# Second normalised tile transposed by a SyncE DMA instead of by TensorE, in a gated two-layer kernel on one core

## What is computed

```python
x = x + tanh(g_xattn[0]) * xattn(layernorm(x), token_ids, ctx, ctx, ctx)
x = x + tanh(g_ffn[0]) * ffn(layernorm(x), Wr, br, Wd, bd, Wu, bu)
# xattn: each token goes to one of 4 experts e, by its token id:
#   y = (silu(h @ W[e].T) * (h @ W[e].T)) @ W[e].T,   W = ctx, 4 x 512 x 512
# ffn: 8 experts of rank 16, the best 2 of softmax(h @ Wr + br) mixed:
#   out = sum_e w[e] * (relu(h @ Wd[e] + bd[e]) @ Wu[e] + bu[e])
```

## Time and profile before

| | us |
|---|---|
| median of 3 runs | 203.06 (202.65 to 203.64) |
| span of the profiled execution | 201.4 |
| busy: TensorE, VectorE, ScalarE, GpSimd | 175.0, 155.7, 111.9, 99.7 |
| share of the span: TensorE, VectorE, ScalarE, GpSimd | 87%, 77%, 56%, 50% |

### The profile page before, as it was taken

The page is one execution under the profiler, slowest core; times in us unless marked ns, Lnnn a source line. Parts: engine busy times, 40 slices in busy tenths (PEclk is TensorE's granted clock), DMA queues, the critical chain, the costliest instruction groups (busy, mean ns, idle before and its releaser), DMA issues.

```text
span 201.4 us, 4382 instructions
## 1 busy us (share of the span) xinstructions
PE 175.0 (87%) x1074; PEld 104.0 (52%) x1075; DVE 155.7 (77%) x523; ACT 111.9 (56%) x224; POOL 99.7 (50%) x246
## 2 busy tenths in 40 slices
PE   1576896999997989999999999999999999976560
PEld 1564463655553656656656556655665655534310
DVE  4859696697768799889888998797877878678640
ACT  2596599884287166473665726547265561545200
POOL 4478846427246366375553735516244162445641
PEclk9999999999999999999999999999999999999955
DMA  5947572101210201203101011011010100101121
GB/s 135 370 163 231 205 216 69 52 5 20 86 55 0 52 0 52 59 0 104 55 0 54 0 52 52 2 52 52 0 54 0 52 20 33 52 0 55 52 104 52
DMA packets 6784, 13.43 MB, mean 67 GB/s; under 512 B 2392, under 2 KB 2520, under 8 KB 6768
## 3 DMA queue, kind: packets, MB, share of 16 engines
q0 software_dynamic: 2560, 8.39, 12.6%
q1 hardware_dynamic: 4208, 4.86, 7.3%
HBM read 9.06 MB, written 4.19 MB: 66 GB/s over the span
## 4 chain that ended last, share of the span: by engine, by line
PE 44%; issue 18%; POOL 10%; DVE 9%; DMA 7%; ACT 4%; DVEq 3%; SPq 2%; POOLq 1%; ACTq 0%
PE ps_y L603 6%; PE ps_y L605 6%; PE ps_y L604 6%; PE ps_a L603 4%; PE ps_a L605 4%; PE ps_a L604 4%; DMA xs<-in_x_dram,rows_of 4%; ACT h L796 3%; POOL rs L457 3%; PE ps_h2T L685 2%; PE ps_pT L624 2%; DMA bu_nat<-in_L_ffn_bu_dram 2%; POOL hot_slot L432 2%; PE ps_hT L677 2%; POOL xs L439 2%
## 5 line engine op out<-in xcount | busy, mean ns | idle before, releaser
L456 POOL TENSOR_SCALAR ve<-mv 128x1 f32<-128x1 f32 x32 | 7.7, 239 | 62.6 <-DVE mv L1099 51.8
L796 ACT ACTIVATE h<-xs,mrs,rs 128x512 f32<-128x512 f32 (+1 forms) x16 | 21.1, 1317 | 22.4 <-POOL mrs L458 22.4
L783 ACT ACTIVATE pT_hi<-ps_pT 128x512 f16<-128x512 f32 x19 | 11.3, 595 | 36.0 <-PE ps_pT L624 36.0
L603 PE MATMUL ps_y<-w_hi,pT_hi 128*128 x76 | 28.8, 379 | 2.3 <-DVE w_lo L952 1.5
L603 PE MATMUL ps_a<-w_hi,hT_hi 128*128 x76 | 29.1, 382 | 0.7 <-DVE hT_lo L1074 0.6
L604 PE MATMUL ps_a<-w_lo,hT_hi 128*128 x76 | 29.1, 382 | 0.0
L605 PE MATMUL ps_a<-w_hi,hT_lo 128*128 x76 | 29.0, 381 | 0.0
L604 PE MATMUL ps_y<-w_lo,pT_hi 128*128 x76 | 28.8, 379 | 0.0
L605 PE MATMUL ps_y<-w_hi,pT_lo 128*128 x76 | 28.8, 379 | 0.0
L1086 DVE SCALAR_TENSOR_TENSOR xs<-ps_y,y_t,xs 128x512 f32 x19 | 14.3, 750 | 10.2 <-PE ps_y L605 7.7
L529 POOL DMA_INDIRECT out_dram<-xs,rows_of x16 | 17.3, 1083 | 5.9 <-DVE xs L1117 3.5
(11 more groups left out here) (209 smaller groups left out, 424.0 us busy)
## 6 DMA issues: line engine op xcount, KB each, us to landing
w_nat<-in_ctx_dram SPq DMA_DIRECT2D x4, 1024.0 KB, 7.9
xs<-in_x_dram,rows_of POOLq DMA_INDIRECT x16, 3.6
wd_nat<-in_L_ffn_Wd_dram SPq DMA_DIRECT2D x1, 256.0 KB
wu_nat<-in_L_ffn_Wu_dram SPq DMA_DIRECT2D x1, 256.0 KB
out_dram<-xs,rows_of POOLq DMA_INDIRECT x16, 2.9
b_in<-in_L_ffn_bd_dram SPq DMA_DIRECT2D x1, 64.0 KB
bu_nat<-in_L_ffn_bu_dram SPq DMA_DIRECT2D x3, 16.0 KB
tok_i<-in_itok_BxS_dram SPq DMA_DIRECT2D x1, 8.0 KB, 1.8
```

The costliest lines, as they stand in the source:

```text
L603: mm(ps[:, :], lhs_hi[:, kc, :], hi, start=(kc == 0), stop=False)
L796: a(h2[:, :, :], x1[:, col(k), :].rearrange("p o (q c) -> p c (o q)", c=KC), ACT.Identity, bias=mrs[:, 1, col(k)], scale=rs[:, 1, col(k)]) ...
```

## The change

`h2` is written in token order, as one 512-wide row a token. ScalarE copies it to fp16 into the first half of a new tile `h2_parts`, VectorE writes the rest into the second half; both read SBUF now. A single DMA transpose, issued by SyncE, brings all eight 128 x 128 blocks of `h2_parts` into `h2T`, whose halves are `h2T_hi` and `h2T_lo`. It waits for the lo part, for the hidden product of the tile before (which reads the same `h2T`) and for the landing of the transpose before. The hidden product waits for its landing. TensorE's transposes of h2 go. To match the order, `wr_nat` and `wd_nat` are loaded with rows c*128 + p, `wd_nat` by eight DMAs. In SyncE's loop transpose t - 10 comes behind the `x_in` signal of tile t, from t = 10 on; ten transposes follow the loop.

```diff
-        h2 = sb("h2", [P, KC, P])
-        h2T_hi = sb("h2T_hi", [P, KC, P], fp16)
-        h2T_lo = sb("h2T_lo", [P, KC, P], fp16)
+        h2 = sb("h2", [P, D])
+        h2_parts = sb("h2_parts", [P, 2, D], fp16)
+        h2T = sb("h2T", [P, 2 * KC, P], fp16)
+        h2T_hi, h2T_lo = h2T[:, 0:KC, :], h2T[:, KC:2 * KC, :]
...
+            def transpose_h2(k):
+                sp.wait_ge(h2_lo_done, k + 1)
+                if k:
+                    sp.wait_ge(hid_mm, k)
+                    sp.wait_ge(h2T_landed, 16 * k)
+                sp.dma_start_transpose(h2T[:, :, :], h2_parts[:, :, :].rearrange("p a d -> p (a d)"))\
+                  .then_inc(h2T_landed, 16)
...
-                    sp.dma_start(wr_nat[:, :, :], Wr.rearrange("(p c) e -> p c e", c=KC)).then_inc(s_small, 16)
-                    sp.dma_start(wd_nat[:, :, :, :], Wd.rearrange("e (p c) r -> p e (c r)", c=KC)).then_inc(s_small, 16)
+                    sp.dma_start(wr_nat[:, :, :], Wr.rearrange("(c p) e -> p c e", c=KC)).then_inc(s_small, 16)
+                    for e in range(EF):
+                        sp.dma_start(wd_nat[:, e, :, :], Wd[e, :, :].rearrange("(c p) r -> p c r", c=KC)).then_inc(s_small, 16)
...
+                if t >= 10:
+                    transpose_h2(t - 10)
+            for k in range(T - 10, T):
+                transpose_h2(k)
             sp.wait_ge(s_scatter, 16 * T)
...
-                pe.wait_ge(h2T_lo_done, k + 1)
+                pe.wait_ge(h2T_landed, (k + 1) * 16)
...
-                if some(T, -2 - LATE, i0):
-                    k = i - 2 - LATE
-                    pe.wait_ge(normed2, k + 1)
-                    for c in range(KC):
-                        last = tr(ps_h2T[:, c, :], h2[:, c, :], ident[:, :])
-                    last.then_inc(h2T_done, 1)
...
-                    wait_last(act, h2T_done, k)
-                    a(h2[:, :, :], x1[:, col(k), :].rearrange("p o (q c) -> p c (o q)", c=KC),
+                    wait_last(act, h2_lo_done, k)
+                    a(h2[:, :], flat(x1[:, col(k), :]),
                       ACT.Identity, bias=mrs[:, 1, col(k)], scale=rs[:, 1, col(k)]).then_inc(normed2, 1)
...
-                    act.wait_ge(h2T_done, k + 1)
-                    wait_last(act, hid_mm, k)
-                    a(h2T_hi[:, :, :], ps_h2T[:, :, :], ACT.Copy).then_inc(h2T_hi_done, 1)
+                    act.wait_ge(normed2, k + 1)
+                    if not (isinstance(k, int) and k == 0):
+                        act.wait_ge(h2T_landed, k * 16)
+                    a(h2_parts[:, 0, :], h2[:, :], ACT.Copy).then_inc(h2_hi_done, 1)
...
-                dve.wait_ge(h2T_hi_done, k + 1)
-                v.tensor_tensor(h2T_lo[:, :, :], ps_h2T[:, :, :], h2T_hi[:, :, :],
-                                ALU.subtract).then_inc(h2T_lo_done, 1)
+                dve.wait_ge(h2_hi_done, k + 1)
+                v.tensor_tensor(h2_parts[:, 1, :], h2[:, :], h2_parts[:, 0, :],
+                                ALU.subtract).then_inc(h2_lo_done, 1)
```

More of the change, by code:

```diff
@@ L285, in bass_flamingo_gated_kernel @@
         normed2 = sem("normed2")
-        h2T_done = sem("h2T_done")
-        h2T_hi_done = sem("h2T_hi_done")
-        h2T_lo_done = sem("h2T_lo_done")
+        h2_hi_done = sem("h2_hi_done")
+        h2_lo_done = sem("h2_lo_done")
+        h2T_landed = sem("h2T_landed")
         hid_mm = sem("hid_mm")
@@ L754, in ffn_squares @@
             def ffn_squares():
-                act.wait_ge(s_small, 16 * 8)
+                act.wait_ge(s_small, 16 * (7 + EF))
                 act.wait_ge(s_sq, 1 + E * KC)
@@ L999, in router_bias @@
             def router_bias():
-                dve.wait_ge(s_small, 16 * 8)
+                dve.wait_ge(s_small, 16 * (7 + EF))
                 v.tensor_scalar(b_in[:, ER:HC], b_in[:, ER:HC], BONUS, None, ALU.add)\
```

## The result

The changed kernel takes 255.71 us (median of 4 runs, 253.45 to 257.48) against 203.22 us for the kernel before beside it: a ratio of 1.255 [1.248, 1.262]. The forecast was 256 us. In the rows `h_parts` is the tile `h2_parts`.

What follows compares the result with a forecast made beforehand. TensorE's own work was taken as the main stage's bound, 8.47 us a step. Terms 3.4 + 3.2 + 38.1 + 4.1 + 3.8 = 52.6, plus span 201.4 and 1.6, gave 255.6, say 256 us; range 220 to 335.

Steps and rivals of the forecast that it cites:

- the steps of 11.4 us: Sign in the main stage: hidden products 11.4 us apart, from 7.2 + 0.1 + 4.1, against TensorE's own 8.03.
- loads and first hidden product: Two terms at the front: smaller load pieces shift everything by +3.4 us; the first hidden product waits for its transpose, +3.2.
- thirteen steps: Main stage, first to fourteenth hidden product: 148.2 us instead of 110.1, +38.1 us.
- What bounds: Main stage: TensorE's work is the bound before; the change puts the transfer on its path, with 1.05 us to hide in.
- The step's fixed chain: Main stage, start of one hidden product to end of the next lo part: 7.2 us, plus 0.1 for semaphore hand-overs.
- L, the landing: Time of the transpose DMA from issue to landing, once a tile: 4.1 us, between 1.8 and 7.9.
- The clock: Rival: TensorE's clock falls in the new waits, half or all its path work at 1.2 GHz: 298 or 339 us; chance 0.12.
- Loads: Early stretch: seven more issues on SyncE's queue delay VectorE's router_bias and all behind it, +3.4 us, bounds +1.5 and +6.8.
- Drain: Last two hidden products, 15 and 16, each waiting for its transpose: +4.1 and +3.8 us.
- Eight blocks one after another: Rival: the transfer is served block by block, 1.8 us each, landing in 14.4 us: 420 us; chance 0.12.
- As fast as ordinary transfers: A skill page's claim on transposing DMAs: landing would be the gather's 3.6 us and the time 248 us.
- Hidden transfer, faster: Rival: with a landing under 0.7 us, lo part plus transfer fit in front of TensorE's 8.03 us: 197 us; chance 0.02.

Runs made afterwards that it cites:

- the double transfer: The changed kernel with each transpose sent a second time into a spare tile, the hidden product waiting for both: 287.24 us, run once.
- its control: The kernel before, TensorE's transposes kept, with the hidden product and what follows it one step later and two buffers: 210.37 us, ratio 1.036.
- the split kernel: The changed kernel with two transposes a tile, one of the hi part and one of the lo part, each sent when written: 250.49 us, ratio 1.222.

## Why the prediction was right

The total was right within 0.3 us, and the mechanism held, but that the number fits so well is luck: the landing, which the sum holds sixteen times, was taken 16 us too large in all, and effects that the forecast left out made up for 13.6 of them. Of the signs that it named, TensorE's waits of some 3 us a step and VectorE's wait of 5 came; the steps of 11.4 us came as a mean of 11.2 and at no quiet step, and the full clock did not come. Point by point, in the difference of the two profiled spans (53.9 us):

| term | predicted | measured |
|---|---|---|
| loads and first hidden product | 3.4 + 3.2 | 77.8 - 66.3 = 11.5 |
| thirteen steps | 38.1 | 145.7 - 110.1 = 35.6 |
| drain, two products | 4.1 + 3.8 | (240.97 - 223.50) - (187.71 - 176.40) = 6.2 |
| behind the last product | 0 | 14.3 - 13.7 = 0.6 |

- **What bounds.** Right. TensorE takes the hidden product first in its step, only 1 us lies before it, and the transfer stands there openly. Moving the product away from it removed the wait and 39 us.
- **The step's fixed chain,** 7.2 + 0.1: right. A quiet step is 10.45 us, less 3.1 of landing leaves 7.3.
- **L, the landing: the mis-sized step.** Taken as 4.1 us; measured 3.1 undisturbed. The nearest row, the gather's 3.6, was the better guess, and the additions were not borne out: the data take about 1.5 us, and that is not on top of a gather's time. With 3.1 the sum gives 256 - 16 x 1.0 = 240 us. The kernel with the gathers away and the clock held took 242.1, with the early stretch at 1.2 GHz still in it. So the forecast's mechanism and sum hold, for a transfer that nothing disturbs and a landing of 3.1.
- **What made up for it.** 13.6 us that the forecast did not have: landings of 3.5 to 6.5 us beside four gathers (7.7 us, with the falls of the clock that they bring), and the rest of the clock's falls (5.9 by the medians). I had read the DMA engines' share of 0.11 as room, and didn't ask which transfers would fall next to which.
- **The clock** was a rival at 0.12, as all or nothing in the waits, 298 us or more. It came in part: the granted clock was 0.94 in the stage, and holding it was worth 4 to 6 us where no gather interferes. In the six quiet steps it stayed full through waits of 2.5 us; it fell to 1.2 GHz in or behind the waits of 6.5, 4.3 and 5.7 us, and once behind one of 2.4 (at 192.2 us; that step took 12.0 us). So the length of the wait alone doesn't decide, and no run here settles what does. With a longer landing the clock would have cost more: the double transfer, whose waits are 3.7 to 3.8 us, paid 1.7 us a step for it.
- **Loads.** +3.4 was predicted and the wait ends 35.14 - 31.90 = 3.2 later, right in size, though by two errors: seven more issues took 5.1 us (5.59 from wd_nat's to wu_nat's issue instead of 0.48), not 3.4, but the last load then landed 35.14 - 31.39 = 3.75 us after wu_nat was issued, not 5.0, and wd_nat's issue began 0.5 earlier. Not predicted: TensorE behind it starts at 1.2 GHz for 6.5 us, so that the first hidden product is 6.0 later with the loads alone.
- **Drain.** +6.2 against +7.9; the 1.0 us too much in L stands in each of its two products. With it out the forecast would be 5.9.
- **Eight blocks one after another:** refuted. L was 3.1, not 14.4, and four blocks land in 2.5 against eight in 3.1. The figure of 1309 ns for a 128 x 128 DMA transpose (the Trainium skill, VectorE: DVE Perf Modes, "The three transpose paths") is not borne out as a price per block: eight took 3.1 us. The advice of that page (section "Rules for kernel authors") to use TensorE where the result may go to PSUM did hold in this kernel.
- **As fast as ordinary transfers** (the Trainium skill, Advanced Engine Details and Errata, "X-Bar Transpose (TRN2)"): the trace agrees in the time to landing, 3.1 us against the 3.8 of a gather of the same size.
- **Hidden transfer, faster:** did not come, as L is far over 0.9. When hidden by hand (one step later), it came out 0.7 us under its control, which is within the noise.

## What to carry to other kernels

Count what lies between the producer and the consumer of the moved data before counting the engine time saved: here 0.44 us of TensorE was exchanged for 3.1 us on its path, sixteen times. A transfer that is exposed costs more than its landing when gathers run beside it, or when its wait brings the clock down. Hidden, it was worth less than the later order that hid it. And look at the by-products of a change one by one: token order was worth 2.4 us without any DMA transpose, once the bias no longer waited for loads that it doesn't read.

## What the runs showed of the hardware

- A DMA transpose of 128 x 1024 fp16 in SBUF (eight 128 x 128 blocks) lands in 3.1 us. SyncE's queue is occupied 1.2 to 1.3 us by its issue, for eight blocks and for four alike; a second one behind it adds 1.3 us.
- Beside an indirect gather issued 0.6 to 1.5 us earlier, the same transpose lands in 3.5 to 6.5 us. A scatter issued 1.2 us earlier hardly slows it (147.21: 3.18 us, a scatter issued at 146.00); in the split kernel a transpose of four blocks with a scatter issued 0.3 us ahead of it landed in 4.0 us instead of 2.4 (153.94 us).
- With a packet of a queue called instruction in the last part of its landing, it took 3.4 to 4.8 us instead of 3.1 (five cases; the packet as the cause is not shown).
- Matmuls whose result is thrown away made the kernel 4 to 6 us faster where no gather was beside a transpose (5.9 by the medians, 3.7 by the profiled spans), by keeping the granted clock at 2.4 GHz in the waits.
- Seven of the eight loads of wd_nat, in 64-byte pieces, were issued in 0.51 to 0.59 us each and one in 1.59; the single load in 256-byte pieces took 0.43. Why the one took so long is open.
- An ACTIVATE of 128 x 512 fp32 in SBUF took 1317 ns with the strided access of the kernel before and 816 in token order.

Left open: whether the instruction packets are what makes some transposes land late; why one of the waits of 2.4 us let the clock fall; and how much the hidden transpose is worth with the token order, for which a control is missing.
